# Panels of 1024 consecutive rows, and the normalization of most rows moved between the units of the main loop

## What is computed

```
h    = relu(layernorm(x))
deg  = clip(adj.sum(axis=1), 1);  dis = deg ** -0.5
diffusion = (dis[:, None] * adj * dis[None, :]) @ h - h
norms = max(norm(h, axis=-1), 1e-8)
sim  = h @ h.T / (norms[:, None] * norms[None, :])
attn = softmax(beta * sim * adj, axis=1)
out  = x + diffusion + sigmoid(alpha) * (attn @ h - h)
```

## Time and profile before

| | |
|---|---|
| median of 3 runs | 1920.75 us |
| the profiled execution's own time | 1921.04 us |
| its span, first to last instruction | 1919.1 us |
| busy TensorE, VectorE, ScalarE, GpSimd | 1827.4, 1226.5, 1306.8, 1269.1 us |
| mean granted TensorE clock | 0.991 of full speed |
| first matmul of `cosines(0)` | 90.28 us |
| first and last `masked` (512 of them) | 93.13 and 1453.35 us |
| first and last matmul of the last stage (L726) | 1465.08 and about 1914 us |

### The profile page before, as it was taken

One profiled execution on the slowest core, in us unless ns is written; L12 is line 12 of the kernel. 1 busy time (PEld: TensorE's weight loads), 2 busy tenths in 40 slices (PEclk: granted clock), 3 DMA queues, 4 the chain that ended last, 5 costly groups with the idle time before them and its releaser, 6 DMA issues.

```text
span 1919.1 us, 44747 instructions
## 1 busy us (share of the span) xinstructions
PE 1827.4 (95%) x19602; PEld 1408.7 (73%) x19602; DVE 1226.5 (64%) x1382; ACT 1306.8 (68%) x1262; POOL 1269.1 (66%) x792
## 2 busy tenths in 40 slices
PE   0489999999999999999999999999998999999998
PEld 0366777777777777777777777777777888888887
DVE  6887787787778778777877877787775210111111
ACT  7688898889889888988988898899887000000000
POOL 3099999999999999999999999999883000000000
PEclk9699999999999999999999999999999999999999
DMA  9639887767888877778888767888426755554530
GB/s 177 97 63 135 106 106 101 100 89 102 100 106 101 108 105 89 100 96 100 106 100 109 100 89 100 100 107 100 116 92 239 226 178 182 170 200 165 202 107 12
DMA packets 188455, 229.38 MB, mean 120 GB/s; under 512 B 9316, under 2 KB 164964, under 8 KB 183396
## 3 DMA queue, kind: packets, MB, share of 16 engines
q0 software_dynamic: 135168, 67.13, 45.1%
q1 hardware_dynamic: 25060, 144.71, 20.6%
q10 hardware_dynamic: 28032, 14.69, 3.0%
HBM read 352.32 MB, written 75.50 MB: 223 GB/s over the span
## 4 chain that ended last, share of the span: by engine, by line
PE 93%; ACT 3%; DVE 2%; issue 1%; POOL 1%; DMA 0%; SPq 0%; DVEq 0%; ACTq 0%
PE cos_ps L670 34%; PE top_ps L700 12%; PE top_ps L704 12%; PE cos_ps L726 12%; PE top_ps L726 12%; PE top_ps L702 12%; ACT arena L329 1%; ACT xe L353 0%; POOL hlo L278 0%; POOL ustage L287 0%; PE cos_ps L656 0%; DMA asb<-x_in 0%; DVE ustage L518 0%; DVE ptmp L489 0%; ACT xe L337 0%
## 5 line engine op out<-in xcount | busy, mean ns | idle before, releaser
L287 POOL TENSOR_TENSOR ustage<-xe,ustage 128x1024 f16<-128x1024 f32 x512 | 1094.7, 2142 | 155.3 <-ACT xe L410 148.2
L584 DVE TENSOR_TENSOR xe<-cos_ps,arena 128x1024 f32<-128x1024 f32 x512 | 627.0, 1225 | 286.2 <-PE cos_ps L670 191.5
L406 ACT ACTIVATE ustage<-xe,ebias,ab 128x1024 f16<-128x1024 f32 x512 | 635.3, 1241 | 132.2 <-DVE xe L584 128.8
L700 PE MATMUL top_ps<-h,ustage 128*128 128x129 f16 x4096 | 719.2, 220 | 6.2 <-POOL ustage L287 6.1
L704 PE MATMUL top_ps<-h,ustage 128*128 128x129 f16 x4096 | 718.9, 220 | 0.0
L702 PE MATMUL top_ps<-hlo,ustage 128*128 128x128 f16 x4096 | 718.4, 219 | 0.0
L410 ACT ACTIVATE xe<-xe,ebias,ab 128x1024 f32<-128x1024 f32 x512 | 628.6, 1228 | 5.5 <-POOL ustage L287 4.7
L700 PEld LDWEIGHTS top_ps<-h,ustage 128*128 128x128 f16 x4096 | 400.8, 98 | 75.6 <-POOL ustage L287 15.9
L702 PEld LDWEIGHTS top_ps<-hlo,ustage 128*128 128x128 f16 x4096 | 400.8, 98 | 56.6
L704 PEld LDWEIGHTS top_ps<-h,ustage 128*128 128x128 f16 x4096 | 400.8, 98 | 0.0
L559 DVE TENSOR_REDUCE top_ps<-arena 128x8 f32<-128x1024 uint16 x256 | 311.8, 1218 | 2.0 <-DMA arena<-adj_in_dram 2.0
(11 more groups left out here) (87 smaller groups left out, 1017.5 us busy)
## 6 DMA issues: line engine op xcount, KB each, us to landing
arena<-adj_in_dram POOLq DMA_DIRECT2D x256, 256.0 KB, 8.6
at_scratch<-arena SPq DMA_DIRECT2D x128, 512.0 KB, 3.3
arena<-at_scratch SPq DMA_DIRECT2D x26, 2048.0 KB, 8.9
xe<-at_scratch SPq DMA_DIRECT2D x6, 2048.0 KB, 8.5
h_scratch<-arena SPq DMA_DIRECT2D x4, 1024.0 KB, 7.6
arena<-h_scratch SPq DMA_DIRECT2D x2, 2048.0 KB, 8.8
ustage<-h_scratch ACTq DMA_DIRECT2D x16, 256.0 KB, 3.0
ptmp<-x_in ACTq DMA_DIRECT2D x64, 64.0 KB, 5.0
```

The source lines that it names most:

```text
L287: nc.gpsimd.tensor_tensor(elo[:, n % ES, :], ef[:, n % XS, :], ehi[:, n % ES, :], ALU.subtract).then_inc(elo_done, 1)
L406: nc.scalar.activation(ehi[:, n % ES, :], xm[:, n % XS, :], ACT.Exp, bias=ebias[:, 0:1], scale=ab[:, 1:2]).then_inc(ehi_done, 1)
L584: nc.vector.tensor_tensor(xm[:, n % XS, :], cos_ps[:, n % 2, :], at8[:, m % W, :, n % B], ALU.mult).then_inc(x_done, 1)
L700: nc.tensor.matmul(top_ps[:, bank, col:col + P + 1], head, h1[:, s, 0:P + 1], start=(first and t % 3 == 0), stop=final, skip_group_check=True)
```

## The change

1. **Panels.** Panel p is now rows 1024 p to 1024 p + 1023, whose columns of `uT` come from one group of `x` (half of it). `uT_hi` and `uT_lo` are stored so that these are contiguous, and the tile that `cosines` loads as weights is read with a step of 4 elements (`own`).
2. **One group up front.** Before the loop only group 0 is made ready for `cosines` (two half groups of 8 tiles, hb 0 and 1) and half of group 1 is normalized. Groups 2 and 3 of `x` are loaded by SyncE once the first adjacency chunk is there; GpSimd issues three chunks after group 0 of `x` has landed, where it issued two after all of `x`.
3. **The other groups in the loop.** Their statistics, roots, relu, fp16 heads, tails and transposes stand between units 1 and 68, at places given by unit number. VectorE scales the half groups to unit length (`late_unit_rows`), TensorE transposes them in fp32 into the free slot of `cos_ps` (`transposed`, 8 per half group, at the units in `AHEAD`), and VectorE splits on the way out (`copy_uT`). At those units `cosines(n)` waits for `masked(n - 1)`, and `cosines(n + 1)` for `copy_uT`. `late_root` and its like keep one operand in PSUM.
4. **Shared groups.** The chunks of the first two panels alternate (`ORDER`), so the sums of panel 0 and 1 are each made in two runs (`RUNS`): ScalarE copies the first run out, VectorE adds the second to it (`add_acc`, at units 98 and 130).
5. **Roots.** Square root and `reciprocal` give way to an exponential of the number's bits (`rough_root`) and three Newton steps, 9 dependent VectorE instructions. ScalarE so stays with one function table.
6. **Squares.** The sum of squares of h comes from `bn_stats` (VectorE) instead of a square on ScalarE and a sum on VectorE.
7. **After the loop.** The degrees are brought into both layouts by a small matmul (`degrees_to_tiles`), and their rough root is taken at unit 510 on ScalarE, before the loop ends. h is scaled and split in pieces of 4 tiles, not 8. Loads and stores of the output are 2 DMAs where there were 10 and 8.

The lines that carry this:

```diff
+    AHEAD = {10: 2, 13: 3, 49: 4, 52: 5, 65: 6, 68: 7}
+
+    ORDER = [(0, 0), (1, 0), (1, 1), (0, 1), (0, 2), (0, 3), (1, 2), (1, 3)] + [(p, ch) for p in range(2, PANELS) for ch in range(CH)]
+
+    RUNS = [(0, 0, 1), (1, 1, 3), (0, 3, 6), (1, 6, 8)] + [(p, CH * p, CH * (p + 1)) for p in range(2, PANELS)]
+    RUN_OF = {k: r for r, (p, k0, k1) in enumerate(RUNS) for k in range(k0, k1)}
...
     x_v = x.rearrange("(ch q w c b) d -> ch q c w (b d)", ch=CH, q=Q, w=W, c=C, b=B)
-    out_v = out.rearrange("(ch q w c b) d -> b w q c ch d", ch=CH, q=Q, w=W, c=C, b=B)
-    adj_v = adj.rearrange("(y w c b) j -> b w c y j", y=CH * Q, w=W, c=C, b=B)
+    x_again_v = x.rearrange("(p t r) d -> p r t d", t=PT, r=P)
+    out_v = out.rearrange("(p t r) d -> p r t d", t=PT, r=P)
+    adj_v = adj.rearrange("(p a c) j -> p c a j", a=32, c=C)
...
+            sp.wait_ge(rows_loaded[0], 16 * 8)
+            for g in range(2, CH):
+                for q in range(Q):
+                    load_x(g, q)
...
-                               ).then_inc(rows_loaded[k % RS], 16)
-
-
+
+
+            pool.wait_ge(x_loaded[0], 16 * Q)
...
+            tails = {6: 4, 8: 5, 10: 6, 12: 7, 46: 8, 48: 9, 50: 10, 52: 11, 60: 12, 62: 13, 64: 14, 66: 15}
...
+            def rough_root(root, value):
+
+                half = 0.5 * 0.6931471805599453
+                return nc.scalar.activation(root, value.bitcast(mybir.dt.int32), ACT.Exp, scale=-half / 2 ** 23, bias=bits_bias[:, 0:1])
+
...
-                    copy_acc(n // TILES - 1)
+                run = RUN_OF[(n - LAG) // 16] if n >= LAG else 0
+                if n >= 16 and n - LAG + 1 == 16 * RUNS[run][2] and run not in (2, 3):
+                    copy_acc(run)
...
+                if n in (3, 5, 44, 46, 57, 59):
+                    head_of_h({3: 2, 5: 3, 44: 4, 46: 5, 57: 6, 59: 7}[n])
+                elif n in (6, 45, 61):
+                    ssq_root({6: 1, 45: 2, 61: 3}[n])
+                elif n == 33:
+                    var_root(2, 2)
+                if 35 <= n < 43:
+                    relu(2, 2 * (n - 35), 2 * (n - 34))
+                elif 48 <= n < 56:
+                    relu(3, 2 * (n - 48), 2 * (n - 47))
+                if n == UNITS - 2:
+                    act.wait_ge(deg_in_place, Q)
+                    rough_root(dis2[:, :], degs[:, :]).then_inc(deg_root, 1)
 
...
+            def refine_root(value, root, tmp, to):
+
+                for step in range(3):
+                    link(nc.vector.scalar_tensor_tensor(out=tmp, in0=value, scalar=-0.5, in1=root, op0=ALU.mult, op1=ALU.mult))
+                    link(nc.vector.tensor_tensor(tmp, tmp, root, ALU.mult))
+                    last = nc.vector.scalar_tensor_tensor(out=root if step < 2 else to, in0=tmp, scalar=1.5, in1=root,
+                                                          op0=ALU.add, op1=ALU.mult)
+                    if step < 2:
+                        link(last)
+                return last
 
...
+            def late_unit_rows(hb):
+                of = slice(8 * hb, 8 * (hb + 1))
+                dve.wait_ge(rnorm_ready, hb // 2 + 1)
+                if hb > READY:
+                    dve.wait_ge(uT_done, hb)
+                link(nc.vector.tensor_copy(late_ps[:, 0:8], rnorm[:, of]))
+                nc.vector.tensor_tensor(unit[hb], x_st[:, of, :], late_ps[:, 0:8].unsqueeze(2).to_broadcast([P, 8, P]),
+                                        ALU.mult).then_inc(u_ready, 1)
+                dve.wait_ge(u_ready, hb + 1)
...
+                lo = uT_lo[:, of].rearrange("d (w y b) -> d w b y", w=2, b=B)
+                link(nc.vector.tensor_copy(hi, src))
+                nc.vector.tensor_tensor(lo, src, hi, ALU.subtract).then_inc(uT_copied, 1)
+
+            stats_of_x(0, 0, 16)
...
+            early_shift(1)
+            stats_of_h(0, 8, 16)
+            early_square_sums(0)
+            early_norms(0)
+            stats_of_h(1, 0, 8)
+            copy_uT(0, 0)
+            copy_uT(1, 1)
 
             def turn(m):
...
+                    of = slice(t0 + 3 * k, t0 + 3 * k + n)
+                    last = nc.vector.tensor_tensor(asb[:, of, 0:P + 1], top_ps[:, k, 0:n * HS].rearrange("p (t d) -> p t d", d=HS)[:, :, 0:P + 1],
+                                                   asb[:, of, 0:P + 1], ALU.add)
+                last.then_inc(acc_added, 1)
 
...
-                if n >= 0:
-                    masked(n)
+            for n in range(UNITS):
+                if n in AHEAD:
+                    copy_uT(AHEAD[n], (slot_of(n) + 1) % 2)
+                masked(n)
+                if n in (16 * RUNS[2][2] + LAG - 1, 16 * RUNS[3][2] + LAG - 1):
+                    add_acc(2 if n < 16 * RUNS[3][2] else 3)
...
+
+                if 1 <= n < 5:
+                    stats_of_h(1, 2 * n + 6, 2 * n + 8)
+                elif 16 <= n < 32:
+                    g, o = 2 + (n - 16) // 8, (n - 16) % 8
+                    stats_of_x(g, 2 * o, 2 * (o + 1))
+                    if o == 7:
+                        link(mean_var(g))
+                elif 37 <= n < 45:
+                    stats_of_h(2, 2 * (n - 37), 2 * (n - 36))
+                elif 53 <= n < 61:
+                    stats_of_h(3, 2 * (n - 53), 2 * (n - 52))
+                if n == 32:
+                    nc.vector.tensor_scalar(va[:, 32:TILES], mv[:, 32:TILES, 1], LN_EPS, None, ALU.add).then_inc(var_ready, 1)
+                elif n == 34:
+                    late_shift()
+                elif n in (5, 44, 60):
+                    late_square_sums({5: 1, 44: 2, 60: 3}[n])
+                elif n in (7, 46, 62):
+                    late_norms({7: 1, 46: 2, 62: 3}[n])
+                elif n in (8, 11, 47, 50, 63, 66):
+                    late_unit_rows({8: 2, 11: 3, 47: 4, 50: 5, 63: 6, 66: 7}[n])
...
+            def transposed(hb, slot):
+                pe.wait_ge(u_ready, hb + 1)
+                for t in range(8):
+                    last = nc.tensor.transpose(cos_ps[:, slot, t * P:(t + 1) * P], unit[hb][:, t, :], ident32[:, :])
+                last.then_inc(uT_done, 1)
+
+            def own(uT, s):
+                return uT[:, :].rearrange("d (x y b) -> d x b y", y=P, b=B)[:, s // B, s % B]
...
+                if n in AHEAD:
+                    pe.wait_ge(x_done, n)
+                elif n - 1 in AHEAD:
+                    pe.wait_ge(uT_copied, AHEAD[n - 1] + 1)
+                elif n >= 2:
...
+                    if n in AHEAD:
+                        pe.wait_ge(x_done, n - 1)
+                        transposed(AHEAD[n], (slot_of(n) + 1) % 2)
```

More of the change, by code:

```diff
@@ L312, in _ @@
         def _(act):
-            for g in range(CH):
+            for g in range(2):
                 for q in range(2, Q):
@@ new lines, in var_root, with relu @@
+            def var_root(g, groups=1):
+                of = slice(16 * g, 16 * (g + groups))
+                act.wait_ge(var_ready, g + 1)
+                rough_root(vb[:, of], va[:, of]).then_inc(std_ready, 1)
+            def relu(g, first, last):
+                act.wait_ge(ln_ready, min(g, 2) + 1)
+                for s in range(16 * g + first, 16 * g + last):
+                    nc.scalar.activation(x_st[:, s, :], x_st[:, s, :], ACT.Relu, scale=rstd[:, s:s + 1],
+                                         bias=shift[:, s:s + 1]).then_inc(relu_done, 1)
@@ L393, in copy_acc @@
+            relu(1, 8, 16)
+            def copy_acc(run):
+                panel, _, behind = RUNS[run]
+                act.wait_ge(attn_done, 16 * behind)
+                if run in (0, 4):
+                    groups = 1 if run == 0 else CH
+                    for g in range(groups):
+                        act.wait_ge(h_kept[g], 16 * Q)
+                    act.wait_ge(hlo_ready, 4 * groups)
+                    act.wait_ge(u_ready, 2 * groups)
                 t0 = panel * PT
@@ L535, in _, with late_root @@
-            square_sums(2)
-            norms(2)
-            split(1)
-            copy_uT(1)
-            square_sums(3)
-            split(2)
-            norms(3)
-            copy_uT(2)
-            split(3)
+                refine_root(ssq[:, of], vb[:, of], vc[:, of], rnorm[:, of]).then_inc(rnorm_ready, 1)
+            def late_root(value, root, tmp, to):
+                near = late_ps[:, 0:value.shape[-1]]
+                link(nc.vector.tensor_copy(near, root))
+                for step in range(3):
+                    link(nc.vector.scalar_tensor_tensor(out=tmp, in0=value, scalar=-0.5, in1=near, op0=ALU.mult, op1=ALU.mult))
+                    link(nc.vector.tensor_tensor(tmp, tmp, near, ALU.mult))
+                    last = nc.vector.scalar_tensor_tensor(out=near if step < 2 else to, in0=tmp, scalar=1.5, in1=near,
+                                                          op0=ALU.add, op1=ALU.mult)
+                    if step < 2:
+                        link(last)
+                return last
@@ L684, in degrees @@
[L684 to L691 removed]
```

(11 more changed lines are left out.)

484 lines of the change are left out of this document (239 added, 245 removed).

## The result

The changed kernel takes 1914.11 us (median of 7 runs, 1912.24 to 1918.02), the kernel before 1920.75 (7 runs). The ratio is 0.9966, 95% interval 0.9955 to 0.9978: faster by 6.6 us, where 18.7 were forecast. 1914.11 lies inside the range of 1887 to 1917, outside the forecast's own range of 1895 to 1912.

A forecast was written before the change was run, and what follows sets the result against it. TensorE was taken to set the pace in the loop, with little slack on three other engines, and to idle before it. 1921.0 - 50.3 + 31.1 + 3.0 - 2.5 = 1902.3 us, forecast 1902; range for 8 in 10: 1887 to 1917.

The forecast's parts named there:

- Copying out in two VectorE passes is priced like `masked`, 2 x 1.225: Start and loop: each VectorE pass copying a transposed half group out of PSUM takes 1.225 us, two per half group.
- Start: Before the loop: masked(0) starts at 42.9 us instead of 93.13, a gain of 50.3, bounds 43 and 52.
- Loop: masked(0) to masked(68), with the moved work: 215.6 us, 31.1 more than before.
- The larger engine's excess alone: Units 0 to 68: counting only the busiest engine's overload per stretch loses 29.8 us, the lower bound; 37.5 was taken.
- the first rival: Loop: moved work hides better, 29.8 us lost instead of 37.5, one `add_acc` hidden; about 1893 us, chance 17%.
- Later: Loop after unit 68: two `add_acc` on VectorE and additional runs cost 3.0 us, bounds 1 to 6.
- After the loop: Last stage starts 1.8 us sooner, one output DMA saves 0.7: together 2.5 us, bounds 0 and 6.
- without that blocking the last sums would set it: gain 4.5: End of loop: were Newton steps not held by GpSimd's subtractions, the last stage would gain 4.5 us instead of 1.8.
- Weights, chunks: Loop and start: stepped weight loads hide beside matmuls, cost 0; adjacency chunks served in order are never late.
- the second (the lower clock in the waits): Loop: TensorE drops to its lower clock in six waits, at 1.8 to 2 us each; 1914 us, chance 7%.
- a wait of 1.86 us at full clock: Reason against the lower-clock rival: a row with TensorE 1.86 us idle at full clock, no expected wait being much longer.
- a clock under 0.95 between 50 and 260 us: Loop's first units: a granted TensorE clock this low was named as a sign that the forecast is wrong.

The follow-up runs named there:

- e1: Changed kernel with the copies of half groups writing packed fp16 and reading PSUM with a step of 128 fp32 elements: 1892.58 us, 0.9858 of the kernel before.
- e2: Changed kernel with transposes writing every fourth fp32 column of PSUM, so both copy passes are packed: 1892.14 us, 0.9855 of the kernel before.
- e7: e2 with 127 of 128 columns of relu left out in units 35 to 42 and 48 to 55: 1890.20 us, 0.9841 of the kernel before.
- e4: Changed kernel with the Newton steps after the loop keeping one operand in PSUM: 1909.5 us, 0.9947 of the kernel before.
- e6: e2 with cosines' weights read as 128 consecutive columns, from other rows than needed: 1893.02 us, 0.9855 of the kernel before.
- e3: Changed kernel with the subtraction of every half group's copy done twice: 1940.41 us, 1.0107 of the kernel before.

## Why the prediction was wrong

The direction, the two stages that change and the overlap in each were right in the main. The step that failed is "Copying out in two VectorE passes is priced like `masked`, 2 x 1.225": the term was mis-sized. A pass takes 2.45 us. The row it was priced from has packed fp32 output, the new pass an fp16 output with 8 bytes from one number to the next, which no row of before shows. For the transposes, which no row showed either, the prediction gave a bound from each side, but not here; it looked at the step only where the weights are read. A bound of twice the price would have put 1922 into the range. A second thing was put at nothing: TensorE's lower clock in the loop, 1.7 to 3.4 us of which came with the longer waits alone (see the rivals below).

Point by point, with e1 and e2 as the kernel in which that term is as priced:

- Start. All else held: masked(0) at 42.77 against 42.9, transposes 1.9 each, chunk 0 on time. In the changed kernel two half groups add 4.6.
- Loop. Forecast 215.6, e2 208.5, the changed kernel 223.6. By stretches, e2 against the forecast: units 0 to 13 43.3 against 44.6; 14 to 31 48.8 against 48.7; 32 to 46 44.7 against 48.2; 47 to 56 31.8 against 33.5; 57 to 67 39.9 against 40.6. In units 0 to 13 e1 has 44.1, of which more below. The larger miss, 5.2 us, is in units 32 to 56, in which ScalarE's load was added to VectorE's in part. The larger engine's excess alone was reckoned there at 4.9 and 5.1 us and measured at 5.0 and 5.3, ScalarE's in units 32 to 46 and VectorE's in 47 to 56 (e7); over all 68 units it was reckoned at 29.8 and measured at 30.4. This is the first rival's mechanism, and its 1893 is what e1 and e2 take; in the changed kernel the dearer passes hide it.
- Later. `add_acc` and the additional runs were taken at 3.0, and the stretch as a whole takes no longer: 1175.6 us in e2, 1175.68 before. Where both `add_acc` stand, from masked(98) to masked(132), it is 91.28 us against 90.17, so they cost about 1; the units before are 0.9 shorter and those behind 0.3. The 1.7 of the changed kernel are not a wait, since TensorE is idle for 0.25 us there; they are the lower clock right behind masked(68), shown below.
- After the loop. Taken 1.8 and 0.7, measured 1.3 and 0.8. That the steps are blocked by GpSimd is shown by e4, and "without that blocking the last sums would set it: gain 4.5" too: 11.73 to 7.41 is 4.3. The block came nearly as priced: two steps were held, each until GpSimd's subtraction of 2.1 us ended, and the root was ready 7.79 us after the last masked, where 7.65 were reckoned. The other 0.3 are the scaling and the split, 2.61 us from there to the last stage instead of 2.3. This is what the Trainium skill says in SBUF — State Buffer, section Who interferes with whom: the later one waits for the whole of the other, whatever that lasts. The trace agrees: 2.03 and 2.10 us beside instructions of 2.12 and 2.26, 1.04 beside one of 1.117.
- Weights, chunks. Priced 0 and found 0 (e6; no wait before `turn(0)`).

So 1902.3 less 0.1, 7.1 and 3.1 that were reckoned too much, and 0.4 too little at the end, is 1892.4, what e1 and e2 take; the mis-sized term, with the clock that it brought, adds 21.4 and gives 1913.8. Two errors of opposite sign: the forecast would have been 10 us too high had the passes been as priced.

Of the rivals, the second (the lower clock in the waits) named 1914, and the measured time is 1914.1. That is luck in the main, but its cause has a share. Two places show it, in which TensorE waits for nothing. From masked(14) to masked(32) the changed kernel takes 50.6 us, e4, whose loop is the same, 48.9, and so do e1 and e2. From masked(68) to masked(98) the changed kernel and e4 take 80.3, e1 and e2 78.5. Windows of the changed kernel and of e4 behind masked(14), then of the changed kernel and of e2 behind masked(68):

```profile
96.00:102.00 6.00, 6.00 (x58) 4.74 (x57) 3.34 (x3) 4.54 (x4) 4.28 (x2) 0.83 0.22 87
96.00:102.00 6.00, 6.00 (x68) 4.49 (x66) 4.73 (x5) 5.80 (x6) 4.84 (x3) 1.00 0.23 90
272.00:278.00 6.00, 6.00 (x54) 4.70 (x53) 4.56 (x5) 4.66 (x4) 3.22 (x3) 0.72 1.00 149
252.00:258.00 6.00, 6.00 (x65) 4.37 (x64) 5.02 (x5) 5.47 (x5) 5.16 (x5) 1.00 1.09 82
```

TensorE is busy for all 6 us in each, and at the lower clock gets through 58 matmuls where it otherwise does 68, and 54 instead of 65. Each place costs 1.7 us. Ahead of both it had waited for a copy, 3.1 and 2.9 us. Where VectorE is what TensorE waits for, a slower matmul lies partly in the wait: in the first 14 units e1, with this window, takes 44.1 us, and e2, at a clock of 1.00, 43.3.

```profile
60.00:80.00 20.00, 17.17 (x178) 12.63 (x176) 18.12 (x26) 14.79 (x14) 14.71 (x9) 0.91 1.19 173
```

So of the 21.4 us between the two profiled executions about 17 are the longer passes themselves and about 4 the clock: 1.7 + 1.7, in places where no run with packed passes has it low, and 0.8, which those runs have too, e2 excepted. In e4 the first of the 1.7 is missing, though TensorE waited as long there (3.1 us); what decides that is open, and the loop of one kernel takes 221.7 us in one execution and 223.6 in another by it. The rival's six times 1.8 to 2 us are nearly three times too much. The prediction's reason against it, a wait of 1.86 us at full clock, did not reach as far as the waits of 2.3 to 3.1 us that came; the sign that it named, a clock under 0.95 between 50 and 260 us, is there even in e2 (0.91 from 211 to 251 us).

The clock also cost 1.8 us in the last stage, which the prediction left unchanged and e4 took back. The Trainium skill, TensorE: Matmul & The Clock Gate, section Why this matters for your kernels, asks for short idle gaps; this case agrees at the end of the loop, where the gap of 2.84 us cost 1.8, and in the loop for some of the waits only, 1.7 us each.

## What to carry to other kernels

- Price a VectorE pass by its output pattern too, not by its column count alone, and when the trace shows no such write, put the doubled cost into the range. Where a layout has to be interleaved, let the reader of PSUM or TensorE's write do the stepping, not the narrow write to SBUF.
- When moved work is spread over units, take the excess of the busiest engine in each stretch. Adding a second engine's load overstated it by 5 us here; work added to the engine that sets those units costs nearly its full length, and more when TensorE's clock falls behind the longer waits (e3 has such windows).
- Where a time that should repeat differs by 1 to 2 us while TensorE is busy throughout, look at the granted clock of the two executions before looking for a wait.
- Small dependent steps beside a long GpSimd instruction should keep one operand in PSUM.

## What the runs showed of the hardware

- A write of fp16 numbers 8 bytes apart by VectorE takes 2.42 to 2.47 us for 1024 columns, a packed one 1.21 to 1.23; a PSUM read with a step of 128 fp32 numbers costs nothing (1.21 to 1.23), and neither does a transpose written to every fourth fp32 column of PSUM (1.94 and 1.97 us for eight, 1.94 and 1.86 packed).
- An fp32 transpose of 128x128 takes 0.23 to 0.25 us (1.86 to 1.97 for eight), near the 1.9 read from the degree product.
- Stepped fp16 weights load in 114 ns, packed ones in 98, with no effect on the unit.
- A VectorE step with both inputs in SBUF was held for 1.7 to 1.8 us by GpSimd twice, and never with one of them in PSUM.
- Behind waits of TensorE of 2.9 and 3.1 us in the changed kernel its granted clock was 0.72 and 0.83 in windows of 6 us, which cost 1.7 us each time; behind the same wait of 3.1 us in e4 it was 1.00. Two gaps of 0.64 and 1.10 us at the end of e4's loop left it at 1.00.
- A ScalarE activation of one column takes 373 ns, one of 128 columns 480.
